# Cross-attention with a quantised FFN on one core: values multiplied in two row halves, and the second tile's exponential taken head by head from the scores

## The reference, cut to what matters

```python
q, k, v = LN(x) @ Wq, ctx @ Wk, ctx @ Wv           # heads of 32 columns
q, k = rope(q), rope(k)
attn = softmax(q @ k.T / sqrt(32))                 # 512 x 77 per batch and head
x1 = x + mean_over_heads(attn @ v) @ Wo
scale = max(abs(LN(x1))) / 127
out = x1 + round(LN(x1) / scale) @ ternary(W).T * w_scale * scale + bias
```

## Time and profile before

| | us |
|---|---|
| median of three runs | 1268.39 |
| the profiled execution, its own time | 1268.9 |
| its span, from the first to the last instruction | 1267.0 |
| TensorE busy, of the span | 1201.2 (95%) |
| VectorE busy | 1124.7 (89%) |
| ScalarE busy | 1001.1 (79%) |
| GpSimd busy | 794.2 (63%) |
| mean granted TensorE clock | 0.991 |

### The profile page before, as it was taken

How to read it: one execution, slowest core, us unless ns; L and a number is a source line. 1 busy time by engine, 2 the same in 40 slices (tenths; PEclk the granted TensorE clock), 3 DMA queues, 4 the chain that set the end, 5 groups by cost and what they waited for, 6 DMA issues and landing times.

```text
span 1267.0 us, 42077 instructions
## 1 busy us (share of the span) xinstructions
PE 1201.2 (95%) x12408; PEld 983.0 (78%) x12471; DVE 1124.7 (89%) x2410; ACT 1001.1 (79%) x2339; POOL 794.2 (63%) x1536
## 2 busy tenths in 40 slices
PE   7999999999999999999999999999789999999997
PEld 7998888888888888888888888888645555555554
DVE  4656999999999999999999999999878888888887
ACT  4566888888888888888888888888768888888886
POOL 4767898898998988989989889899700000000000
PEclk9999999999999999999999999999889999999999
DMA  9772555555555555555555543323029999999945
GB/s 291 225 205 66 160 178 169 173 173 170 164 178 166 178 168 175 170 174 162 182 163 181 164 123 94 87 84 84 2 99 398 403 396 398 399 408 396 395 206 212
DMA packets 97241, 260.26 MB, mean 205 GB/s; under 512 B 42538, under 2 KB 53994, under 8 KB 76723
## 3 DMA queue, kind: packets, MB, share of 16 engines
q1 hardware_dynamic: 97154, 259.75, 59.6%
q10 hardware_dynamic: 48, 0.07, 0.0%
HBM read 137.11 MB, written 122.64 MB: 205 GB/s over the span
## 4 chain that ended last, share of the span: by engine, by line
DVE 44%; PE 35%; issue 15%; DVEq 3%; ACT 1%; POOL 1%; DMA 0%; SPq 0%; POOLq 0%; ACTq 0%
DVE amax L903 10%; PE pT_ps L1265 10%; PE sc_ps L1265 9%; DVE x_sb L940 8%; DVE mx_sb L918 7%; DVE bn_sb L930 6%; DVE e_sb L922 6%; PE qo_ps L1069 5%; PE xT_ps L1256 5%; DVE bn_sb L910 3%; PE sc_ps L1263 2%; DVE mv_sb L947 2%; DVE rinv_sb L890 2%; PE xT_ps L1058 1%; PE pT_ps L1263 1%
## 5 line engine op out<-in xcount | busy, mean ns | idle before, releaser
L1210 PE MATMUL qo_ps<-wqs,xT_sb 128*128 128x128 f32 x2048 | 262.6, 281 | 0.9 <-ACT xT_sb L700 0.9
L1210 PEld LDWEIGHTS qo_ps<-wqs,xT_sb 128*128 128x128 f32 x2048 | 238.2, 191 | 21.5 <-issue 20.0
L1233 PEld LDWEIGHTS pT_ps<-v_blk,pT_sb 103*128 103x128 f32 x1536 | 197.3, 190 | 11.8 <-ACT pT_sb L712 0.9
L940 DVE SCALAR_TENSOR_TENSOR x_sb<-x_sb,mv_sb,xT_ps 128x512 f32 (+1 forms) x256 | 180.0, 745 | 25.5 <-DVE bn_sb L930 10.8
L1233 PE MATMUL pT_ps<-v_blk,pT_sb 103*128 103x136 f32 x1536 | 200.1, 280 | 0.3 <-ACT pT_sb L712 0.3
L1008 DVE TENSOR_TENSOR x_sb<-x_sb 128x512 f32 (+1 forms) x256 | 164.7, 684 | 1.2 <-ACT x_sb L758 1.2
L700 ACT ACTIVATE xT_sb<-xT_ps 128x512 f32<-128x512 f32 x256 | 139.1, 595 | 33.3 <-PE xT_ps L1136 28.9
L663 ACT ACTIVATE sq_sb<-x_sb 128x512 bf16 (+1 forms) x256 | 162.4, 634 | 0.6 <-DVE x_sb L940 0.2
L903 DVE TENSOR_REDUCE amax<-x_sb (+1 forms) x128 | 154.6, 1208 | 0.3 <-issue 0.3
L758 ACT ACTIVATE x_sb<-pT_ps,mean,cols 128x512 f32<-128x512 f32 x128 | 99.5, 777 | 63.6 <-PE pT_ps L1265 63.6
L1265 PE MATMUL pT_ps<-wT,x_sb 128*128 128x512 f16 x512 | 131.4, 379 | 3.2
(11 more groups left out here) (135 smaller groups left out, 2673.7 us busy)
## 6 DMA issues: line engine op xcount, KB each, us to landing
out_y<-x_sb SPq DMA_DIRECT2D x112, 1024.0 KB, 6.5
x_sb<-in_x SPq DMA_DIRECT2D x128, 512.0 KB, 3.9
x_sb<-out_y SPq DMA_DIRECT2D x48, 1024.0 KB, 8.9
x_sb<-in_ctx SPq DMA_DIRECT2D x38, 256.0 KB, 4.0
k_blk<-k_scr SPq DMA_DIRECT2D x256, 9.6 KB, 1.7
v_scr<-x_sb SPq DMA_DIRECT2D x38, 68.0 KB, 3.0
k_scr<-x_sb SPq DMA_DIRECT2D x38, 64.0 KB, 3.3
v_blk<-v_scr SPq DMA_DIRECT2D x128, 10.2 KB
```

The source lines that it names most:

```text
L940: dve.scalar_tensor_tensor(out=x1_at(kj, gj, t), in0=x_sb[:, kj // 2, 2 * (kj % 2) + t, :], scalar=mv_sb[:, kj, t, 0:1], in1=bank[t][:, :] ...
L1210: last = pe.matmul(bank[2][:, t * HD:(t + 1) * HD], xT_sb[:, t, c, :], wqs[:, c, :], start=c == 0, stop=c == EC - 1)
L1233: last = pe.matmul(bank[6][:, t * HEADS * VC:(t + 1) * HEADS * VC], pT_sb[0:CR, t, c * P:(c + 1) * P], v_blk[0:CR, slot, c, :, :].rearrang ...
```

## The change

It does the following things, all in stage 2 except where said.

1. **Values by halves.** v_blk holds two heads in the rows 0 to 63 and two in the rows 64 to 127 (rows h%2 x 26 for a head's 26 key rows, columns in three chunks). The values are 12 matmuls in the code for 6 before, each of 64 rows and 68 columns; the one half of the rows writes bank 0, the other bank 1. A key a lies in chunk a % 3, so the transpositions of the exponentials read every third column of e_sb (128 of them) where they read 103 adjacent ones. e_sb grows to 2 x 192 columns per tile, with zeros between the heads. Value DMAs are four per batch instead of six.
2. **The values' product is moved** from VALUE at the end of a TensorE step to HEAD at the start of the next step, and its result from pT_ps to sc_ps, the banks of the scores. The transposed queries and output also go to sc_ps. So TensorE begins each step with a wait for exp_done of the step before, and the scores wait for pv_copied and oT_copied; ScalarE's copy of the values waits for qT_done and oT_done too.
3. **The output product** has banks of its own (y_ps), is float32 with 64 rows per tile (both tiles beside each other in the two halves of the rows), and comes before the projection. ost_sb and its two GpSimd operations go; its transpositions are 2 instead of 4. The transposition of x waits for q_copied instead of added_t, the projection writes bank 0.
4. **The second tile's exponential.** VectorE subtracts the maximum for the first tile only. For the second it computes nb = -(maximum x scale), four numbers per row, and ScalarE takes four exponentials of 77 columns each, from the scores in PSUM, with the scale and nb as pointers. ScalarE does all exponentials before it copies q, where it did them after.
5. **VectorE's and GpSimd's order.** bn_stats goes to either side of the residual, bn_aggr and the variance move one step later (to ROPE), amax behind the residual additions. GpSimd's power for the scale moves between the two parts of the rotation, the second one ahead of the sums of the heads.
6. **Constants** (stage 1): three memsets more (wst, o_sb, e_sb), Wo loaded twice instead of four times, four VectorE operations for wst instead of five, one row more of v_scr stored.

The core of the diff:

```diff
@@ sync @@
-                for c, r, n, h, a in segs:
-                    sp.dma_start(v_blk[r:r + n, k % 2, c, h, :], v_scr[bass.ds(b * CTX + a, n), h, :])\
+                for h in heads:
+                    row = h // 2 * HALF + h % 2 * HR
+                    sp.dma_start(v_blk[row:row + HR, k % 2, :, h % 2, :],
+                                 v_scr[bass.ds(b * CTX, CHUNKS * HR), h, :].rearrange("(r c) v -> r c v", c=CHUNKS))\
@@ gpsimd @@
-                    pool.tensor_tensor(ost_sb[:, :, :, 0, :],
...
-                    pool.tensor_tensor(ost_sb[:, :, :, 1, :],
...
@@ scalar @@
                     act.wait_ge(pv_done, j + 1)
+                    if score:
+                        act.wait_ge(qT_done, score[0] + 1)
+                    if resid:
+                        act.wait_ge(oT_done, resid[0] + 1)
...
                 if stat:
                     square(0)
+                if score:
+
+                    j, kj, gj = score
+                    act.wait_ge(rs_ready, j + 1)
+                    act.wait_ge(sub_done, j + 1)
+                    act.activation(probs_of(kj % 2, 0), probs_of(kj % 2, 0), ACT.Exp,
+                                   scale=rs_sb[:, kj, 0:1])
+                    act.wait_ge(nb_ready, j + 1)
+                    for h in range(HEADS):
+                        last = act.activation(probs_of(kj % 2, 1)[:, h // 2, h % 2, :],
+                                              scores_of(1)[:, h // 2, h % 2, :], ACT.Exp,
+                                              bias=nb_sb[:, kj % 2, h:h + 1], scale=rs_sb[:, kj, 1:2])
+                    last.then_inc(exp_done, 1)
                 if proj:
...
-                    act.activation(q_sb[:, :], bank[2][:, 0:2 * HD], ACT.Copy).then_inc(q_copied, 1)
-                if score:
-
-                    j, kj, gj = score
-                    act.wait_ge(rs_ready, j + 1)
-                    for t in range(2):
-                        act.wait_ge(sub_done_t, 2 * j + t + 1)
-                        act.activation(e_sb[:, kj % 2, t, :], e_sb[:, kj % 2, t, :], ACT.Exp,
-                                       scale=rs_sb[:, kj, t:t + 1]).then_inc(exp_done_t, 1)
+                    act.activation(q_sb[:, :], bank[0][:, 0:2 * HD], ACT.Copy).then_inc(q_copied, 1)
@@ vector @@
+                    dve.wait_ge(mx_ready, 2 * j + 1)
+                    dve.tensor_tensor(probs_of(kj % 2, 0), scores_of(0),
...
+                    dve.wait_ge(rs_ready, j + 1)
+                    dve.wait_ge(mx_ready, 2 * j + 2)
+                    dve.tensor_scalar(nb_sb[:, kj % 2, :], mx_sb[:, 1, :], rs_sb[:, kj, 1:2], -1.0,
+                                      ALU.mult, ALU.mult).then_inc(nb_ready, 1)
@@ tensor @@
+                if score or resid or head:
+
+                    at_least(pe, exp_done, min(i - SCORE, NP_) if isinstance(i, int) else i - SCORE)
+                if head:
...
+                    pe.wait_ge(pT_copied_t, 2 * j + 2)
+                    for t in range(2):
+                        for c in range(CHUNKS):
+                            for n in range(2):
+                                rows = slice(n * HALF, (n + 1) * HALF)
+                                last = pe.matmul(sc_ps[:, n, t * 2 * VC:(t + 1) * 2 * VC],
+                                                 pT_sb[rows, t, c * P:(c + 1) * P],
+                                                 v_blk[rows, slot, c, :, :].rearrange("p h v -> p (h v)"),
+                                                 start=c == 0, stop=c == CHUNKS - 1)
+                    last.then_inc(pv_done, 1)
...
                     for t in range(2):
-                        for c, start in enumerate(STARTS):
-                            last = halves(pT_ps, (t * CHUNKS + c) * HALF, e_sb[:, kj % 2, t, start:start + CR])
+                        for c in range(CHUNKS):
+                            last = halves(pT_ps, (t * CHUNKS + c) * HALF, e_sb[:, kj % 2, t, c::CHUNKS])
...
-                    at_least(pe, sub_done_t, 2 * j)
+                    if head:
+                        pe.wait_ge(pv_copied, head[0] + 1)
+                    if resid:
+                        pe.wait_ge(oT_copied, resid[0] + 1)
                     pe.wait_ge(qT_copied, j + 1)
...
+                    for t in range(2):
+                        rows = slice(t * HALF, (t + 1) * HALF)
+                        last = pe.matmul(y_ps[:, t, :], oT_sb[rows, :], wst[rows, :], start=True, stop=True)
+                    last.then_inc(y_done, 1)
                 if proj:
...
-                        pe.matmul(bank[t][:, :], oT_sb[:, t, :], wst[:, :], start=True, stop=True)\
-                          .then_inc(y_done_t, 1)
-                if value:
...
-                    pe.wait_ge(pT_copied_t, 2 * j + 2)
```

More of the change, by code:

```diff
@@ L49 @@
 CHUNKS = 3
-CR = -(-SC // CHUNKS)
-STARTS = [c * CR if (c + 1) * CR <= SC else SC - CR for c in range(CHUNKS)]
+HR = -(-CTX // CHUNKS)
+EP = CHUNKS * HALF
 CROWS = B * CTX
@@ L350, in _ @@
                 elif n == 3:
-                    for m in range(1, 4):
-                        sp.dma_start(wo4[D * m:D * m + D, :], wo).then_inc(wo_rest_in, 16)
+                    sp.dma_start(wo4[HALF:HALF + D, :], wo).then_inc(wo_rest_in, 16)
                 elif n == 5:
@@ L381, in v_fetch @@
                 at_least(sp, pv_done, 2 * (b - 2) + 2)
-                v_step(b, k, SEGS)
+                v_step(b, k, range(HEADS))
             sp.wait_ge(zeroed, ZEROED)
@@ L421, in _ @@
                         k_step(b, b)
-                    elif first < j <= first + 3:
-                        v_step(b, b, SEGS[(j - first - 1) * 2:(j - first) * 2])
+                    elif first < j <= first + 2:
+                        v_step(b, b, range((j - first - 1) * 2, (j - first) * 2))
             for n in range(ORING):
@@ L1148, in step @@
                     for t in range(2):
-                        last = halves(qo_ps, t * HALF, qr_sb[:, kj % 2, t * HD:(t + 1) * HD])
+                        last = halves(sc_ps, SC + t * HALF, qr_sb[:, kj % 2, t * HD:(t + 1) * HD])
                     last.then_inc(qT_done, 1)
@@ L1153, in step @@
                     j, kj, gj = resid
-                    held(ost_ready, j + 1, ost_count, 1)
-                    for t in range(2):
-                        last = halves(qo_ps, P + t * HALF,
-                                      ost_sb[:, t, :, :, :].rearrange("p a b d -> p (a b d)").bitcast(F32))
-                    last.then_inc(oT_done, 1)
+                    held(o_ready, j + 1, o_count, 1)
+                    halves(sc_ps, SC + P, o_sb[:, :, :].rearrange("p t d -> p (t d)")).then_inc(oT_done, 1)
                 if proj:
                     j, kj, gj = proj
-                    pe.wait_ge(x_in[kj], gj * 16 + 16)
-                    if isinstance(j, int) and j <= RESID:
-                        at_least(pe, xT_copied_t, 2 * j)
-                    else:
-                        held(added_t, 2 * (j - RESID), added_count, 2)
+                    if not isinstance(j, int) or j > 0:
+                        held(q_copied, j, q_count, 1)
                     for t in range(2):
@@ L1207, in step @@
                     for t in range(2):
[L1208 removed]
                         for c in range(EC):
[L1210 removed]
+                            last = pe.matmul(bank[0][:, t * HD:(t + 1) * HD], xT_sb[:, t, c, :], wqs[:, c, :],
                                              start=c == 0, stop=c == EC - 1)
                     last.then_inc(q_done, 1)
[L1213 to L1222 removed]
@@ L1223, in step @@
-                if value:
-                    j, kj, gj = value
-                    slot = kj // 2 % 2
-                    if kj % 2 == 0:
-                        pe.wait_ge(v_in[slot], gj * (2 * V_DMAS * 16) + (kj // 4 + 1) * (V_DMAS * 16))
-                    pe.wait_ge(pT_copied_t, 2 * j + 2)
-                    for t in range(2):
-                        for c in range(CHUNKS):
-                            last = pe.matmul(bank[6][:, t * HEADS * VC:(t + 1) * HEADS * VC],
-                                             pT_sb[0:CR, t, c * P:(c + 1) * P],
-                                             v_blk[0:CR, slot, c, :, :].rearrange("p h d -> p (h d)"),
-                                             start=c == 0, stop=c == CHUNKS - 1)
-                    last.then_inc(pv_done, 1)
```

217 lines of the change are left out of this document (106 added, 111 removed).

## The result

The changed kernel takes 1370.82 us (median of four runs, 1370.15 to 1375.4) against 1268.05 for the kernel before: a ratio of 1.0818, 95% interval 1.0794 to 1.0842. It is slower by 102.8 us; 1397 was forecast, with 1315 to 1463 as the range.

The account below looks back on a forecast made before the run. The prediction took a loop of VectorE and TensorE to bound the kernel at 6.27 us a step; a new loop through ScalarE, 2.14 + 5.15 = 7.29 us, adds 128.5 us over 126 steps, giving 1397 us, range 1315 to 1463.

Parts of the forecast that it names:

- What bounds the kernel before: Kernel before: a loop of VectorE and TensorE sets the 6.27 us step, VectorE closes it, and ScalarE has slack.
- its wait of 0.74 us: ScalarE's wait per step for the projection (for q) in the kernel before, taken as harmless idle time.
- The new loop: From exp_done over the values' product, ScalarE's copies and exponentials to the next exp_done: 7.29 us a step against 6.27.
- First half: The new loop from exp_done over TensorE's values, transposed queries and output to ScalarE's first copy: 2.14 us.
- the projection's 0.113 us for a pair: Time taken for each of the values' 12 matmul pairs, from the projection's instructions of similar form: 1.36 us in all.
- the rival at 0.065 a pair: Row tiling pays in full: value pairs at 0.065 us, loop 6.71 us, 1324 us; chance 0.13.
- Second half: The new loop on ScalarE, from its first copy to exp_done, including 1.48 us for four small exponentials: 5.15 us.
- hidden, but barely: Scores, maxima and first subtraction take 3.17 us, just before ScalarE is ready for the first exponential at 3.23.
- a forecast difference of 0.06 us: Between the path over scores and VectorE, 3.17 us, and ScalarE's own queue, 3.23, up to the first exponential.
- The sum: 126 steps growing from 6.27 to 7.29 us add 128.5 us to 1268.9, giving 1397.
- The strided read: Exponentials' transpositions reading columns 12 bytes apart: forecast to cost 0; as a rival stalling the scores, 1479 us, chance 0.06.
- TensorE's loop of 6.43: TensorE's own loop per step if ScalarE were quick: 6.43 us, covered by the 7.29 us loop, yet above 6.27.

Follow-up runs that it names:

- e4: The kernel before with part 5's order alone (bn_aggr and variance one step later, GpSimd's power moved): 1242.87 us, 0.9795 of the kernel before.
- e2: The kernel before with part 4 alone, the second tile's exponential taken head by head from the scores: 1296.47 us, 1.0222 of the kernel before.
- e5: The changed kernel with a spare 512-column copy on ScalarE behind the second square, where it waits for TensorE: 1374.95 us, one run, step 7.02 us.
- e8: The changed kernel with ScalarE's first square moved from ahead of the exponentials to behind them: 1372.77 us, one run, step 7.02 us.
- e9: The changed kernel with the exponentials' transpositions reading 128 adjacent columns instead of every third one (wrong values, for timing): 1373.69 us, one run.
- e6: The changed kernel with a spare 512-column copy on ScalarE ahead of the exponentials: 1418.25 us, one run, step 7.39 us.
- e1: The changed kernel with part 4 undone, one 308-column exponential for the second tile and VectorE subtracting its maximum: 1300.05 us, 1.024 of the kernel before.
- e7: The changed kernel with the values' product in free columns of pT_ps, ahead of the wait for exp_done (some columns left out): 1327.05 us, one run.
- e3: The changed kernel with 34 instead of 68 moving columns in the values' product (every second head left out): 1386.32 us, one run.
- e10: The kernel of e1 with the exponentials' transpositions reading 128 adjacent columns instead of every third one: 1297.22 us, one run.

## Why the prediction was right

**What bounds the kernel before.** Right that VectorE closes the step, as far as e4 shows it, whose edit is on VectorE and GpSimd together. Wrong to read ScalarE's slack from its wait of 0.74 us: e2 added 0.75 us to ScalarE, only some 0.54 of it found room, and the wait stayed at 0.68. What ScalarE waits for there itself waits for ScalarE's earlier work.

**The new loop.** Right, and shown: its length is unmoved by ScalarE's total work (e5), by its work beside the path (e8) and by TensorE's work beside it (e9); it grows with work on it (e6) and falls when a piece leaves it (e1, e7).

**First half.** 2.14 us forecast, 0.24 + 1.39 + 0.55 = 2.18 measured in the turn above, and 2.08 in the mean of the steps between 300 and 800 us. The choice of the projection's 0.113 us for a pair was right (1.39/12 = 0.116 with the switch), and the rival at 0.065 a pair, 1324 us, didn't come. A quarter of the moving columns of the kernel before, on half the rows, took 1.36 us for 1.48 (e3). The Trainium skill, TensorEngine Tiling (Array Packing), Theoretical Speedup, has up to twice the speed for a contraction of 64 rows or fewer, and this product didn't show it. The Trainium skill, TensorE: Matmul & The Clock Gate, LDWEIGHTS, has a load's time go by its columns and not its rows. For this product e3 agrees; for transpositions the columns alone don't decide, as the 0.062 to 0.117 us a pair of the last section show.

**Second half.** 5.15 us forecast. In the turn above ScalarE's first copy starts at 499.25 and the exponentials end at 504.29, 5.04 us; the mean of the same steps is 4.98. Two terms were too large: four exponentials cover 1.31 us, not 1.48 (they last 0.41 and start 0.30 apart, not 0.43 and 0.35), and the values' copy holds ScalarE for 0.29, not 0.44, since the old distance held a wait of the copy behind it. Together 0.32 us, or 126 x 0.32 = 40 us. Part of it comes back in a wait that the forecast had as "hidden, but barely": ScalarE waits for the subtraction, so the square holds it for 0.87 us in this turn (501.65 to 502.52), not 0.62. And the half runs over the scores, not down ScalarE's queue; at a forecast difference of 0.06 us this changed no number, but e8 shows that it would have misled anyone who then trimmed ScalarE there.

**The sum.** 0.75 us a step instead of 1.02: 95 us instead of 128.5. The mechanism held, and the size of a step's growth was a third too large. The forecast left out the end: 10.2 us more from the last rotation to the end of the span, in part at the low clock (last section). With both counted, 1268.9 + 95.3 + 1.1 + 10.2 = 1375.5, which is the profiled execution; 1397 was 26 above the median. That it came so near is partly luck, for what was left out ahead of and behind the steps made up for 11 of the 33 us by which the steps were overestimated.

**Off the path.** The strided read costs more than before (0.117 a pair for 0.09, within the bounds) and nothing in time, shown by e9. TensorE's loop of 6.43 was e1's 6.47. The 31.4 us by which e1 is above the kernel before weren't divided among the other parts. If part 5's order gave its 25.8 us (e4) there too, which no run shows, the rest would cost some 57. All that is shown of it is that e7 has the product's place in the loop worth at least 0.34 us a step while the four exponentials are there.

## What to carry to other kernels

Before moving an operation, write down the ring of waits that it will stand in, across all engines, and add up one turn; it can grow by 0.75 us a step while every engine gets a smaller busy share. An engine's idle time is room for more work only as far as the thing waited for doesn't depend on that engine's own earlier work; to find out, put a spare instruction there and another elsewhere, and see which of them costs. Look first for reorderings that drop an engine's wait for its own last result: here that, with one move on GpSimd, was worth 2% alone.

## What the runs showed of the hardware that was not expected

- **Weight reads with a distance.** Transposing 64 x 64 pieces with 128 weight columns 12 bytes apart takes 0.117 us a pair from start to start (e_sb in the changed kernel: the 0.86 us that the six pairs cover less one instruction of 0.273, over five). The same measure gives 0.062 with adjacent columns (e10, the same operation on the same tile, instructions of 0.222) and 0.096 with 103 adjacent columns (the kernel before, 0.73, instructions of 0.251). A load lasts 205 ns in the first case and 138 in the second. So 128 adjacent columns were faster here than 103, and the number of columns alone doesn't decide.

```profile
L1152 PEld LDWEIGHTS pT_ps<-ident,e_sb x10: 189/205/208, 499.9 to 506.9; 64*128 64x128 f32 x10
```

```profile
L1150 PEld LDWEIGHTS pT_ps<-ident,e_sb x12: 137/138/140, 505.4 to 505.7; 64*128 64x128 f32 x12
```

- **Two pointers and small tiles.** 77-column exponentials with scale and bias as pointers last 0.41 us and start 0.30 apart: the overlap of neighbours is 0.11 us, not the 0.08 that the 512-column copies showed.
- **The clock at the end of the pipeline.** Behind the last rotation of the changed kernel TensorE is busy 22.37 of 32.30 us and the granted clock averages 0.62, that is, it ran at 1.2 GHz for most of it and at 2.4 for the rest; in the kernel before it was busy 17.12 of 24.00 us there, at 0.79. In e3, where TensorE does the same number of instructions with fewer columns, the clock also fell in the middle of the pipeline. Windows of the changed kernel, then of the kernel before:

```profile
991.70:1024.00 32.30, 22.37 (x184) 15.12 (x182) 18.87 (x40) 17.47 (x53) 12.82 (x27) 0.62 0.01 2
```

```profile
895.00:919.00 24.00, 17.12 (x139) 12.94 (x137) 20.15 (x41) 17.60 (x50) 16.26 (x35) 0.79 0.01 1
```
